# A graph network, a linear-attention mixer and a slice attention on one core: a staged beginning, input scales from one chain, and edge blocks with one more step of slack

## The reference, cut to what matters

```python
xn = layernorm(x)                                   # x: 6250 nodes x 256
gnn = graph_attention(xn, src, dst, edge_weight)    # 4 heads of 64; 100000 edges
#   score = a_s[src] + a_d[dst] + aw_e*weight + ab; w = exp(-relu(score/20))
#   out[n] = sum over edges with src = n of w*feats[dst] / sum of w
mix = four layers of: x += linear_attention(ln1(x)); x += gelu(ln2(x) @ W1 + b1) @ W2 + b2
x = x + gnn + mix
x = x + slice_attention(layernorm(x))   # softmax((h@W_x + b_x)@W_slice + b_slice)/temp, 8 heads x 64
```

## Time and profile before

| | |
|---|---|
| profiled execution | 3684.8 us, span 3683.0 us, granted TensorE clock 0.954 of full |
| median of three runs | 3684.2 us |
| TensorE matmul busy | 3311.6 us (90%) |
| VectorE busy | 2372.1 us (64%) |
| GpSimd busy | 1964.2 us (53%) |
| ScalarE busy | 1162.7 us (32%) |
| chain that ended last | PE 56%, DVE 24%, POOL 7%, DMA 6%, issue 5% |

### The profile page before, as it was taken

The page is one execution under the profiler, slowest core; times in us unless marked ns, Lnnn a source line. Parts: engine busy times, 40 slices in busy tenths (PEclk is TensorE's granted clock), DMA queues, the critical chain, the costliest instruction groups (busy, mean ns, idle before and its releaser), DMA issues.

```text
span 3683.0 us, 43892 instructions
## 1 busy us (share of the span) xinstructions
PE 3311.6 (90%) x13948; PEld 2347.1 (64%) x13948; DVE 2372.1 (64%) x6185; ACT 1162.7 (32%) x2070; POOL 1964.2 (53%) x1745
## 2 busy tenths in 40 slices
PE   5888889999899999989997998888899987679979
PEld 3566556667667777757765666766666665455656
DVE  6887889944534444444457877766767765559941
ACT  2333233333333333323333333234334343212210
POOL 2110001777777777777765777747777776400000
PEclk8999999999999999999998999999999999889989
DMA  2322111222312222322234555545555557712134
GB/s 84 121 95 93 37 34 45 44 49 41 87 36 47 47 47 44 70 55 47 48 97 111 144 146 139 153 131 152 157 145 165 148 152 121 96 34 84 65 113 151
DMA packets 226435, 338.51 MB, mean 92 GB/s; under 512 B 52502, under 2 KB 180009, under 8 KB 225956
## 3 DMA queue, kind: packets, MB, share of 16 engines
q0 software_dynamic: 67840, 119.33, 17.0%
q1 hardware_dynamic: 120452, 161.93, 13.6%
q10 hardware_dynamic: 37920, 54.45, 4.8%
HBM read 247.40 MB, written 87.29 MB: 91 GB/s over the span
## 4 chain that ended last, share of the span: by engine, by line
PE 56%; DVE 24%; POOL 7%; DMA 6%; issue 5%; ACT 1%; DVEq 1%; SPq 0%; ACTq 0%
PE bank_v L1629 14%; PE bank_a L1614 11%; POOL arena L730 7%; PE bank_e L1671 6%; PE bank_v L1559 3%; PE bank_a L1531 3%; PE bank_v L1519 3%; PE bank_a L1461 3%; PE bank_v L1689 3%; PE bank_v L1602 3%; PE bank_v L1779 2%; DMA arena<-edge_weight_parts 2%; DMA arena<-gather_table,arena 2%; DVE arena L1093 2%; DVE st L965 2%
## 5 line engine op out<-in xcount | busy, mean ns | idle before, releaser
L761 POOL DMA_INDIRECT edge_records<-acc x800 | 969.6, 1212 | 621.1 <-issue 621.1
L730 POOL DMA_INDIRECT arena<-gather_table,arena x880 | 927.7, 1054 | 377.6 <-issue 258.9
L1629 PE MATMUL bank_v<-W_sb,gT 128*125 128x256 f32 x3200 | 748.8, 385 | 1.1 <-issue 1.1
L1614 PE MATMUL bank_a<-hT,W_sb 128*128 128x500 f32 (+1 forms) x1664 | 714.6, 577 | 4.2 <-issue 2.4
L1629 PEld LDWEIGHTS bank_v<-W_sb,gT 128*125 128x125 f32 x3200 | 593.3, 190 | 107.9 <-issue 24.1
L1671 PE MATMUL bank_e<-arena 128*125 128x260 f32 x1760 | 478.0, 418 | 83.6 <-DVE arena L1093 78.7
L1614 PEld LDWEIGHTS bank_a<-hT,W_sb 128*128 128x128 f32 x1664 | 318.6, 194 | 310.0 <-issue 291.1
L1671 PEld LDWEIGHTS bank_e<-arena 128*125 128x125 f32 x1760 | 334.6, 200 | 143.6 <-DVE arena L1093 91.8
L786 ACT ACTIVATE gT<-bank_a,cols 128x500 f32<-128x500 f32 (+1 forms) x416 | 275.0, 661 | 442.9 <-PE bank_a L1614 442.2
L786 ACT ACTIVATE hT<-bank_a,cols 128x500 f32<-128x500 f32 (+1 forms) x208 | 145.2, 748 | 501.5 <-PE bank_a L1461 483.7
L1093 DVE TENSOR_TENSOR arena<-arena 128x1024 f32<-128x1024 f32 x220 | 268.1, 1219 | 0.0
(11 more groups left out here) (276 smaller groups left out, 4370.4 us busy)
## 6 DMA issues: line engine op xcount, KB each, us to landing
residual<-xs SPq DMA_DIRECT2D x60, 500.0 KB
xs<-residual SPq DMA_DIRECT2D x60, 500.0 KB
arena<-edge_rows ACTq DMA_DIRECT2D x220, 125.0 KB
queries<-qT_out SPq DMA_DIRECT2D x48, 500.0 KB
qT_in<-queries ACTq DMA_DIRECT2D x39, 500.0 KB
arena<-gather_table,arena POOLq DMA_INDIRECT x880, 3.8
edge_records<-acc POOLq DMA_INDIRECT x800
slice_weights<-arena SPq DMA_DIRECT2D x12, 1000.0 KB, 5.0
```

What stands on the lines that cost most here:

```text
L730: e.indirect_dma_start(g_of(j)[:, i, :], None, table_d, bass.IndirectOffsetOnAxis(ap=node[:, TE * j + i:TE * j + i + 1].bitcast(I32), axis ...
L761: e.indirect_dma_start(rec_d, bass.IndirectOffsetOnAxis(ap=pos_i[:, f:f + 1], axis=0), r3[:, f, :], None).then_inc(d_rec, 16)
L1614: o = e.matmul(b[:, 0:n], W[:, k, f * P:(f + 1) * P], hv[:, k, 0:n], start=k == 0, stop=k == KC - 1)
L1629: o = e.matmul(b[0:R, i % 2 * D:(i % 2 + 1) * D], gv[:, f, i * R:(i + 1) * R], W2_sb[:, f * D:(f + 1) * D], start=False, stop=f == FB - 1 ...
```

## The change

**Blocks.** Rings: NG = 6 gathers, NO = 2 one-hots, NR = 6 of rows and weights (was 5, 5, 4). The sum of a block moves from `edge(j+4)` to `edge(j+5)`; its one-hot is made after its weighing. ACT issues rows and weights of k+3 instead of k+1 in `edge(k)`. **Norms** are cut into moments, scale and apply, each an item of the list; `ln2` of groups 2 and up and `h1` of all but the last are placed between `down` and `up` pieces, and `q_norm` is cut in two. `rsqrt` has one step of third order and one of second in place of three of second. **Both input scales** come from one chain on a pair of columns. **The beginning:** bias split of 264 columns before `feats(0)`, the rest later; the four quarters of the slice weights are items between the first stages; keys and queries of group 0 come before `x_t(1)`; Wqkv and x of group 2 are loaded ahead of the list. **The end:** x for the first two joins is loaded earlier.

```diff
@@ feed_forward_up / feed_forward_down
+            if f in (1, 2) and s >= 1 and l < LAST:
+                put(0.0, ("h1_scale", "h1_apply")[f - 1], l, s - 1)
...
+            if norm_beside:
+                put(0.0, ("ln2_scale", "ln2_apply")[h], l, s + 1)
@@ the list's beginning
-    for s in range(NGR):
+    put(1.05, "x_t", 0)
+    put(1.15 * GT, "feats", 0)
+    put(1.8, "slice_setup", 0)
+    turn("h1_t", 0, 0)
+    put(1.8, "slice_setup", 1)
+    keys(0, 0)
+    put(1.8, "slice_setup", 2)
+    queries(0, 0)
+    put(0.0, "q_exp", 0, 0)
+    put(1.8, "slice_setup", 3)
+    put(1.05, "x_t", 1)
+    put(0.1, "slice_bias")
+    setup = now()
+    put(0.0, "q_sum", 0, 0)
+    put(0.0, "q_norm", 0, 0)
+    put(1.15 * GT, "feats", 1)
+    for s in range(2, NGR):
...
-    at = 20.0
+    at = setup
...
-    apart = room / (NB + 4)
+    apart = room / (NB + 5)
...
-        NG = 5
+        NG, NO, NR = 6, 2, 6
@@ SP
             load_x(0, 0, x)
-            load_x(0, 1, x)
...
-            e.wait_ge(v_done, v_end("setup"))
-            e.dma_start(wls_d, wls_tmp).then_inc(d_wls, 16)
...
+            load_x(0, 1, x)
             load_qkv(0)
+            load_x(0, 2, x)
...
+                if stage == "slice_bias":
+                    e.wait_ge(v_done, v_end("slice_setup", PAIRS - 1))
+                    e.dma_start(wls_d, wls_tmp).then_inc(d_wls, 16)
...
+                    e.wait_ge(d_flatout, 16 * 9)
+                    e.dma_start(bias3[:, BO:NBIAS], bias_d).then_inc(d_flatin, 16)
...
                 elif stage == "sort" and at[0] == 0:
-                    e.wait_ge(bias_set, 1)
+                    e.wait_ge(slice_bias_set, 1)
@@ SP, down(LAST, 11, 0, 0) and total(11)
+                    elif s == PRE:
+                        load_x(DEPTH + 1, 0, x_d[DEPTH % 2])
...
-                    if s >= NGR - 2:
-                        load_x(DEPTH + 1, s - (NGR - 2), x_d[DEPTH % 2])
+                    if s == PRE:
+                        load_x(DEPTH + 1, 1, x_d[DEPTH % 2])
@@ POOL, edge
-                    elif 4 <= k < NB - 1:
-                        e.wait_ge(e_full[1], k - 3)
+                    elif 5 <= k < NB - 1:
+                        e.wait_ge(e_full[1], k - 4)
                         gather(k + 1)
@@ ACT, edge
-                    for j in (range(2) if k == 0 else range(k + 1, min(k + 2, NB))):
-                        if j >= 4:
-                            e.wait_ge(e_full[0], j - 3)
+                    for j in (range(4) if k == 0 else range(k + 3, min(k + 4, NB))):
+                        if j >= NR:
+                            e.wait_ge(e_full[0], j - 5)
@@ DVE, the chain
-                for k in range(3):
-                    step(e.tensor_tensor(a, y, y, ALU.mult))
-                    step(e.tensor_tensor(a, a, negh, ALU.mult))
-                    o = e.scalar_tensor_tensor(y, a, 1.5, y, ALU.add, ALU.mult)
+                e.tensor_scalar(y15, y, 1.5, None, ALU.mult)
+                step(e.tensor_tensor(a, y, y, ALU.mult))
+                step(e.tensor_tensor(a, a, negh, ALU.mult))
+                step(e.scalar_tensor_tensor(a, a, 5.0 / 3.0, a, ALU.add, ALU.mult))
+                step(e.scalar_tensor_tensor(y, a, 1.25, y15, ALU.add, ALU.mult))
+                step(e.tensor_tensor(a, y, y, ALU.mult))
+                step(e.tensor_tensor(a, a, negh, ALU.mult))
+                return e.scalar_tensor_tensor(y, a, 1.5, y, ALU.add, ALU.mult)
@@ DVE, input_statistics
-                statistics(by_tile(x_of(0, s)[:, :]), nt, stats).then_inc(x_stat, 1)
-                step(e.tensor_tensor(q, y, y, ALU.mult))
-                step(e.tensor_tensor(q, q, var, ALU.mult))
-                step(rsqrt(stats[0:R, 60:60 + nt], q, nt))
+                e.tensor_scalar(negh[:, 0, :], var, 1e-5, -0.5, ALU.add, ALU.mult)
+                step(e.tensor_scalar(negh[:, 1, :], var, -0.5 * (1.0 + 1e-5), -0.5e-10, ALU.mult, ALU.add))
+                rsqrt(yz, negh, both(nwt[0:R, 8:16]), both(nwt[0:R, 16:24])).then_inc(x_stat, 1)
+                step(e.scalar_tensor_tensor(t, negh[:, 0, :], -2.0, yz[:, 0, :], ALU.mult, ALU.mult))
+                step(e.tensor_tensor(yz[:, 1, :], yz[:, 1, :], t, ALU.mult))
@@ DVE, setup and edge_half
+            bias_in_parts(BFEAT, WF).then_inc(bias_set, 1)
...
                     if k < NB:
-                        one_hot(k)
                         one_hot_T(k)
+                    if k >= 3:
+                        one_hot(k - 3)
@@ PE, edge
-                    if k >= 4:
-                        j = k - 4
-                        e.wait_ge(p_set, j + 1)
+                    if k >= 5:
+                        j = k - 5
+                        e.wait_ge(oh_set, j + 1)
```

More of the change, by code:

```diff
@@ L70, in feed_forward_up, with feed_forward_down, norm @@
             put(1.7 * tiles(s) / GT, "up", l, s, f)
-    def feed_forward_down(l, s, i):
+    def feed_forward_down(l, s, i, norm_beside=False):
         for h in range(2):
             put(1.75, "down", l, s, i, h)
+            if norm_beside:
+                put(0.0, ("ln2_scale", "ln2_apply")[h], l, s + 1)
+    def norm(stage, l, s):
+        for part in (stage, stage + "_scale", stage + "_apply"):
+            put(0.0, part, l, s)
     def attend(l, s, i):
@@ L160, in build_program @@
                     turn("ek_t", l + 1, PRE)
-            put(0.0, "h1" if l < LAST else "total", *((l, s - 1) if l < LAST else (s - 1,)))
+            if l == LAST:
+                put(0.0, "total", s - 1)
+            elif s == NGR:
+                norm("h1", l, s - 1)
+            else:
+                put(0.0, "h1", l, s - 1)
             if s < NGR:
@@ L193, in build_program @@
             room += us
-    apart = room / (NB + 4)
+    apart = room / (NB + 5)
     blocks = []
-    for k in range(NB + 4):
+    for k in range(NB + 5):
         blocks.append((k * apart, ("edge", k)))
@@ L384, in build_program @@
         ga += NG * TE * ROW
[L385 to L389, removed]
+        oh_ring = [arena[:, ga + i * TE * R:ga + (i + 1) * TE * R] for i in range(NO)]
+        ga += NO * TE * R
+        ohT_ring = [arena[:, ga + i * BLK // 2:ga + (i + 1) * BLK // 2].bitcast(BF16) for i in range(NR)]
+        last = ga + NR * BLK // 2
         EARLY = 3
@@ L1215, in _ @@
                                     bc(mx.unsqueeze(2), [R, 2 * HM, DH]), ALU.subtract).then_inc(v_done, 1)
[L1216 removed]
+                elif stage == "q_sum":
                     l, s = at
@@ L1486, in _ @@
                 na, nv = a_at[item], v_at[item]
-                if stage == "x_t":
+                if stage == "slice_setup":
+                    q, = at
+                    b = into_v(nv)
+                    e.wait_ge(a_done, a_at[("setup",)] + 1 + q + 1)
+                    for c in range(KC):
+                        e.matmul(b[:, c * P:(c + 1) * P], wxT[:, q, c * P:(c + 1) * P], wsl2, start=True, stop=True)
+                    if q == 0:
+                        e.wait_ge(bx_set, 1)
+                    e.matmul(b[0:3, 256:384], bx3[:, 3 * q:3 * q + 3], wsl2, start=True, stop=True).then_inc(v_full, 1)
+                elif stage == "x_t":
                     s, = at
```

207 lines of the change are left out of this document (110 added, 97 removed).

## The result

The changed kernel takes 3641.7 us, median of four runs (3631.6 to 3644.9), where the kernel before takes 3682.3 beside it (3676.2 to 3685.4): a ratio of 0.9887, 95% interval 0.9863 to 0.9911, 41 us. A set of runs later gave 0.9878 (0.9857 to 0.9898) again. The forecast was 3615 and its range 3572 to 3662, so the sign and the range hold; the gain is 41 us where 70 were forecast. The profiled execution took 3643.8 us, span 3641.7. In three of the five sets of runs even the kernel before took 3821 to 3837 us (the traces of those sets name 46 to 62 waits of GpSimd in the block part "remote", 84 to 108 us in all, those of the other two sets none, and what stands behind them is open), so every run is compared with its own set.

The account below looks back on a forecast made before the run. VectorE was taken to pace the front, TensorE and GpSimd to fill the scatter stretch, GpSimd the blocks. Terms 14 + 18 + 5 + 5 + 17 + 11 = 70 off 3684.8 gave 3615 us; range 3572 to 3662.

Parts of the forecast that it names:

- rivals 1 to 3: Front not reaching the sort, 3651 us (0.17); block loosening does nothing, 3637 (0.09); blocks give more, 3575 (0.14).
- rival 2: Blocks: the loosening does nothing, the ring being freed as before; terms 5 and 17 go, 3637 us; chance 0.09.
- the layer gap: Between layers 2 and 3: TensorE enters and leaves one block earlier, shrinking GpSimd's 38.68 us pause; 5 us, bounds 0 and 6.
- the slow end: Last gathers, from about 3095 us: weights issued two blocks earlier arrive in time; 17 us, bounds 0 and 25.
- the beginning: Front up to the sort: earlier features and x loaded ahead bring sort step 1 forward; 14 us, bounds 5 and 28.
- the join: First join: x loaded some 25 us earlier gives 9 us, shorter norms 2; 11 us, bounds 4 and 13.
- two signs of being wrong: First scatter later than 610 us, or a block period that is not 5.4 to 5.5 us.
- gain 14.7: Sort step 1: from 101.6 to 80 us, less 6.9 us of stage work previously done ahead of it; taken as 14.
- One chain: Input scales: 11 fewer steps of 0.219 us per group, nine groups behind the sort's wait; 18 us, bounds 8 and 22.
- Norms and planner: Front: one rsqrt step fewer per norm, 3 us, and sort steps earlier against the stages, 2; 5 us, bounds 0 and 8.
- rival 4: Blocks: the moved one-hot compare holds one gather per block at 0.45 us, adding 99 us; 3714 us, chance 0.05.
- Eleven shorter norms add 2: Slice part at the first join: eleven norms with a shorter chain add 2 us to the loads' 9.

Follow-up runs that it names:

- e7: Changed kernel with the two input scales found by two separate chains again, as before; 3658.4 us, ratio 0.9937.
- e10: Kernel before with only the one chain for both input scales added; 3819.8 us, before 3837.4 beside it, ratio 0.9962.
- the seven: Seven runs with the changed beginning and chain as they are; their request for W2 is issued at 320.9 to 328.8 us, mean 323.1.
- e5: Changed kernel again with no edit, to stand beside other runs of its set; 3642.7 us, before 3682.4, ratio 0.9878.
- e1: Changed kernel with the block part of before (old rings, sum and weight issue); 3750.9 us, ratio 0.9810, in a set where before took over 3820 us.
- e9: Same kernel as e1, second time: changed kernel with the old block part; 3758.3 us, ratio 0.9800, in a set where before took over 3820 us.
- e12: Same kernel as e1, third time: changed kernel with the old block part; 3762.0 us, ratio 0.9823, in a set where before took over 3820 us.
- e3: Changed kernel with edge lists requested ahead of the flat-bias stores and the blank-record store held until sort step 24; 3728.3 us, before 3820.8, ratio 0.9756.
- e8: Changed kernel with the queue of e6 and unused records naming different nodes in place of node 0; 3594.7 us, ratio 0.9758.
- e6: Changed kernel with SyncE's early queue reordered: flat-bias and blank-record stores later, edge lists right behind the slice weights; 3632.4 us, ratio 0.9862.
- e4: Changed kernel with the join's first two x loads back behind the last total, as before; 3751.1 us, before 3820.8, ratio 0.9800.

## Why the prediction was right, and where it was not

**The number.** The range of 3572 to 3662 us takes in rivals 1 to 3, so it was wide. The forecast's own 3590 to 3640 is missed by 2 us, and the nearest number is that of rival 2, 3637, whose two terms (5 for the layer gap, 17 for the slow end) did come to nothing. That the sum is no further off is in part luck: the beginning gave some 19 us less than forecast and the join 8 more. Of the two signs of being wrong, one held by 1.5 us (first scatter at 608.5, limit 610), and the block period of 5.52 us lies just outside the 5.4 to 5.5 that were named.

**The beginning, predicted 14: wrong.** The two instants came as forecast, TensorE's first feature matmul (22.0 us) and sort step 1 (80.6 us, 80 predicted, wait of 7.65 us, where 10 or more were expected). The step that failed is the one from there to "gain 14.7": I took the time won at sort step 1 as time won for the groups. The x store of group 1 and x of group 4, "queued behind" in `slice_bias` and left "inside the lower bound", were the path. Behind sort step 1 a second wait, 7.56 us for x, let group 4 begin 5.4 us earlier and not 14. And the chain, for which I counted nothing in the groups ahead, explains even these 5.4: e7, without it, begins group 4 at 106.3 us, before at 105.3. From e7 and e10 the term is -3 to -9 us. Where the loss behind group 4 comes from, the runs don't show; in e7 it appears as TensorE's wait for the evicted keys, 21.7 against 9.8 us.

**One chain, predicted 18: right.** 16.4 us (e10) and 19.8 us (e7 against the mean of the seven) in the front, 16 to 22 in the whole by e7. That TensorE would take back some held too: up to 345 us VectorE now waits 14.3 us for TensorE's context product (L1299 for L1631, e5), in e7 4.8, and before not at all.

**Norms and planner, predicted 5.** From the request for W2 to the first scatter it takes 290.8 us before, 285.5 in after and 285.0 in e7: 5.3 us; e10, with the norms and the list of before, takes 292.1. The size agrees; it is a difference of traces, not an experiment on the norms alone.

**Blocks and layer gap, predicted 5: wrong.** The pace was GpSimd's, as forecast: 5.52 us a block, the wait for the weighing gone, TensorE idle nearly as much under another name (174 of 1333 us from the first gather to the last sum, 179 before; L1732 waits 115.3 us for the accumulation, L1660 65.7 before). But the pause shrank from 38.68 to 37.17, by 1.5 and not 5.3, and even that is within the spread: 31.0 to 41.9 us in the eight traces with the new block part, 36.5 to 41.2 in the six with the old. And each gather takes 26 ns longer in the mean, 950.6 - 927.7 = 23 us in all, against 13.6 us less waiting for TensorE: last gather minus first 1308.6 us, 14 more than before. That is rival 4 at a quarter of its price (0.10 us a block, where it decides from 0.32). The mean is 1037 to 1054 ns in the six traces with the old block part and 1064 to 1082 in the eight with the new; but e7, which differs from the changed kernel only in the front, has 1064 and 24 us less from first gather to last, so not all of the 23 us is the block part's.

Here the prediction also read its own rows wrongly. It took a weighing's price for GpSimd to be its full 1.22 us, found 0.45 us a block, and said that the trace does not agree with the full price. Gather by gather the trace does agree. In the earlier trace rows the weighing has 0.70 us to go when the gather starts, and the gather takes 1.52 = 0.70 + 0.82. In after, the weighing has 1.07 us to go and the gather takes 1.88:

```profile
2569.53 1.22 DVE L1139 TENSOR_TENSOR arena<-arena 128x1024 f32<-128x1024 f32 x1
...
2569.68 1.88 POOL L768 DMA_INDIRECT arena<-gather_table,arena  x1 [0.30 <-issue]
```

So it is throughout: of the 193 gathers of before that start with over 0.13 us of a weighing to go, 189 end 0.82 us behind it, to 15 ns; in after 186 of 187. A gather that is already under way when a weighing starts keeps its 0.95 us, and the weighing keeps its 1.22 us. The one-hot compare (0.67 us) does the same: 19 of 19 such gathers before, 60 of 60 in after. A weighing thus costs a gather the part of it that is left when the gather starts, less 0.13 us (0.95 - 0.82); 0.52 us are left in the mean before and 0.58 in after. Of the time by which gathers exceed their median, weighings make up 83.5 us before and 97.2 in after, compares 5.7 and 16.1. So the compare's new place accounts for about 10 of the 23 us, and weighings that meet the gathers earlier for about 14. The Trainium skill, "SBUF — State Buffer", section "Who interferes with whom", has a VectorE instruction with two inputs in SBUF contend with a GpSimd instruction that reads SBUF, by an exclusive lock; the traces agree, for the gather that comes second.

The gain came behind the last gather, where the last sum followed after 24.9 and not 38.2 us, and the two cancel: 1333.5 us from the first gather to the last sum, 1332.8 before. This gain does go with the block part: with the records unspread it is 34.2 to 38.7 us in before, e1, e9, e10 and e12, which have the old one, and 24.9 to 30.8 in e3 to e7.

**The slow end, predicted 17: wrong.** The lower bound had the reason: "if the weights are as late because the gathers fill the engines anyway". The 34.34 us of a weight load was the engines' backlog, not a late request. In after VectorE still waits 19.7 us for weights there (3060 to 3220 us), and 42.5 for gathers, and after the last gather the chain shows 12.60 us of its DMA. I had read the cause in the code, "the padding asks for node 0 each time", and priced the symptom. The cause was worth 38 us (e8 against e6), the largest single gain in this study.

**The first join, predicted 11: too small.** The wait of VectorE is gone, as forecast, and the loads are worth 9.3 us (predicted 9). "Eleven shorter norms add 2" was mis-sized: 6 to 9 us are left for them and for what goes with them. About 3 of these are TensorE's clock. From the transposes of the second join to those of the third it takes 24.4 us before and 21.3 in e4; before, two rows of four matmuls take 3.75 and 3.77 us there in place of 1.98, at a granted clock of 0.50 of full from 3294 to 3302 us (the lower level, 1.2 GHz, behind 9.64 us in which TensorE stood idle), and in e4 one takes 2.92. In the 40 us that start 9.5 us behind the first join's transposes the granted clock is 0.79 before, 0.87 in e4 and 0.87 in after.

**The sum.** -5 and not 14 for the beginning, 18 for the chain, 5, 0, 0 and 19: about 37, against the 41 measured. Against the forecast of 70 the slow end and the blocks lack 22, the beginning 17 to 23, and the join gave 8 more: 31 to 37 less, where 29 less were measured. The chain, the loads of the join and the loss in the beginning rest on runs; the 5 of the norms in front, the rest of the join and the 0 of the blocks are differences of traces.

**A better version.** e8 (spread blank records, queue in order) is faster than both kernels: 3594.7 us, 88 us under before and 48 under the changed kernel.

## What to carry to other kernels

Price the cause, not the symptom: where a queue's packets grow long (0.17 to 0.50 us each), look at the addresses before moving requests ahead, and give padding indices as scattered as the real ones. When work is moved to the front, follow every buffer to the store that frees it: a queue in order carries the delay to a load three groups on. And count what a two-input VectorE operation costs GpSimd by where the gathers start in it, not by its length: a change of order that leaves each engine's work alone can move that price, here by 24 us.

## What the runs showed of the hardware that was not expected

Gathers of 128 rows slow down when all descriptors name one row: 0.50 against 0.17 us of a DMA engine for a packet (e6 and e8), with 93 against 139 GB/s moved in all in those 80 us. A gather that GpSimd starts while the weighing or the one-hot compare runs, both VectorE operations with two inputs in SBUF, takes what is left of that operation and 0.82 us more (before: 208 of 212 such gathers, to 15 ns; after: 246 of 247), and one that started first is not lengthened, nor is the operation (weighings 1.21 to 1.28 us throughout). The mean gather lies between 1037 and 1082 ns by how the two meet, with the same median of 0.95 us.
